# Cross-attention values kept in fp32 as two 64-column tiles, with the output projection inside the loop

## What is computed

```python
x = x + _L0_xattn_ref(_layernorm(x, axis=-1), ctx, ctx, ...)
x = x + _L0_ffn_ref(_layernorm(x, axis=-1), ...)
x = x + _L1_xattn_ref(ctx, _layernorm(x, axis=-1), mask, ...)
x = x + _L1_ffn_ref(_layernorm(x, axis=-1), ...)
# inside _L1_xattn_ref: 16 heads of 64; queries from x, keys and values from x and ctx together
...
out = out.transpose(0, 2, 1, 3).reshape(b, m, h * d)
return out @ Wout + bout
```

## Time and profile before

| what | value |
|---|---|
| median of 3 runs | 2465.91 us |
| profiled execution, its span | 2477.3 us |
| PE busy, weight loads busy | 2096.9 us (85%), 1762.3 us (71%) |
| DVE, ACT, POOL busy | 57%, 46%, 31% |
| the loop of pairs, from the first turn to the last fold | about 735.6 to 1942 us |
| the projection stage behind it | about 1942 to 2023 us |
| mean granted TensorE clock | 0.920 |

### The profile page before, as it was taken

How to read it: one execution, slowest core, us unless ns; L and a number is a source line. 1 busy time by engine, 2 the same in 40 slices (tenths; PEclk the granted TensorE clock), 3 DMA queues, 4 the chain that set the end, 5 groups by cost and what they waited for, 6 DMA issues and landing times. The chain is left out here.

```text
span 2477.3 us, 40299 instructions
## 1 busy us (share of the span) xinstructions
PE 2096.9 (85%) x13062; PEld 1762.3 (71%) x13063; DVE 1409.2 (57%) x3260; ACT 1135.1 (46%) x2179; POOL 764.3 (31%) x733
## 2 busy tenths in 40 slices
PE   5889539997159999999999999999998863799994
PEld 3569535664149988899998898988898753466772
DVE  4370236664638777777778877778877314321223
ACT  3443202221127667666677766666766311222220
POOL 2100002332164443454444444434541000122220
PEclk9898759999569999999999999999999985899997
DMA  5421351111200000000000000000000347111113
GB/s 192 142 85 55 142 190 37 44 47 41 81 20 1 16 17 16 2 16 16 16 16 16 1 16 17 16 17 1 16 10 9 106 152 263 41 34 31 32 34 113
DMA packets 85352, 131.30 MB, mean 53 GB/s; under 512 B 9825, under 2 KB 70943, under 8 KB 83115
## 3 DMA queue, kind: packets, MB, share of 16 engines
q1 hardware_dynamic: 74539, 106.16, 12.6%
q0 software_dynamic: 8320, 20.65, 2.9%
q10 hardware_dynamic: 2304, 2.10, 0.2%
HBM read 87.89 MB, written 40.80 MB: 52 GB/s over the span
## 5 line engine op out<-in xcount | busy, mean ns | idle before, releaser
L1585 ACT ACTIVATE a_probT<-a_slot 128x512 fp32r<-128x512 f32 (+1 forms) x512 | 320.4, 651 | 345.6 <-PE a_slot L1480 343.5
L1639 DVE TENSOR_REDUCE a_part_peak<-a_slot 128x1 f32<-128x512 f32 (+1 forms) x512 | 354.6, 731 | 154.4 <-PE a_slot L1471 150.0
L1686 DVE TENSOR_TENSOR a_probT<-a_slot,a_probT 128x512 fp32r<-128x512 f32 (+1 forms) x512 | 369.6, 753 | 18.2 <-ACT a_probT L1585 15.6
L1471 PE MATMUL a_slot<-a_KHL,a_QHL 128*128 128x512 f32 (+1 forms) x1536 | 337.2, 355 | 20.9 <-DVE a_probT L1686 14.4
L1494 PE MATMUL a_po<-a_probT,a_VHL 128*128 128x256 f32 (+1 forms) x2322 | 339.9, 291 | 11.1 <-DVE a_O L1705 4.4
L1471 PEld LDWEIGHTS a_slot<-a_KHL,a_QHL 128*128 128x128 f32 x1536 | 271.9, 190 | 94.9 <-DVE a_probT L1686 37.9
L1494 PEld LDWEIGHTS a_po<-a_probT,a_VHL 128*128 128x128 f32 (+1 forms) x2322 | 293.2, 189 | 24.6 <-issue 24.6
L1480 PE MATMUL a_slot<-ident,a_prob 128*128 128x128 f32 x2048 | 282.9, 282 | 10.6 <-issue 10.2
L1577 ACT ACTIVATE a_prob<-a_slot,a_npeak 128x1024 f32<-128x1024 f32 x256 | 284.6, 1112 | 1.0 <-DVE a_npeak L1641 1.0
L1480 PEld LDWEIGHTS a_slot<-ident,a_prob 128*128 128x128 f32 x2048 | 221.7, 142 | 11.3 <-issue 10.7
L1420 PE MATMUL a_side<-a_W,a_latT 128*128 128x128 f32 x1536 | 194.7, 281 | 14.1 <-DMA a_W<-in_L_xattn_Wkv_dram 9.6
(11 more groups left out here) (331 smaller groups left out, 3411.3 us busy)
## 6 DMA issues: line engine op xcount, KB each, us to landing
m_up<-_L_ffn_gate_up_proj_dram SPq DMA_DIRECT2D x8, 1024.0 KB
a_o_rows<-a_O SPq DMA_DIRECT2D x16, 512.0 KB, 3.5
a1o_o<-a_o_rows SPq DMA_DIRECT2D x16, 512.0 KB, 3.5
m_up<-in_L_ffn_W_dram SPq DMA_DIRECT2D x8, 1024.0 KB
m_down<-in_L_ffn_W_dram SPq DMA_DIRECT2D x8, 1024.0 KB
a_prob_dram<-a0p_zeros SPq DMA_DIRECT2D x4, 1632.0 KB, 10.6
a_dist_dram<-a_dist SPq DMA_DIRECT2D x4, 1632.0 KB, 8.2
a_band_prob<-a_prob_dram SPq DMA_DIRECT2D x4, 1632.0 KB, 7.0
```

The lines of the kernel that those rows point to most:

```text
L1471: ins = t_.matmul(out[:, lo:hi], q, KHL[:, pair.parity, h, part, lo:hi], start=part == 0, stop=part == 1)
L1585: a_.activation(probT[:, u // 2 % 2, 0, lo:hi, u % 2, :], slot[u % 2][:, lo * P:hi * P].rearrange("p (t q) -> p t q", q=P), ACT.Copy).then ...
L1639: v.tensor_reduce(part[:, i:i + 1], slot[u % 2][:, lo:hi], AX.X, ALU.max).then_inc(part_peaked, 1)
L1686: v.tensor_tensor(pT[:, 1], slot[u % 2][:, lo * P:hi * P].rearrange("p (t q) -> p t q", q=P), pT[:, 0], ALU.subtract).then_inc(probT_low, 1)
```

## The change

Seven edits, all in `layer1_attention` and in the host layout of its weights.

1. Values and turned probabilities are stored once, in fp32 (`V`, `probT`), not as high and low parts. ScalarE copies four of the nine turned blocks (`copy_first`) and VectorE the other five (`copy_rest`), each straight from PSUM; the subtractions go.
2. A group is now four units: two tiles of queries of both heads. `weigh` issues 18 fp32 matmuls of 256 columns: for each key tile one with head 0's 64 columns of values into partitions 0 to 63 of `po_t`, and one with head 1's into partitions 64 to 127. All 18 are issued in two bursts, eight behind the turn of unit u % 4 == 1 and ten behind that of u % 4 == 3, and ahead of the piece. Before, nine were issued with every unit, behind the piece.
3. The fold, `copy_outputs`, `O` and `o_rows` go. The row sums are inverted, widened to 64 columns each on VectorE, transposed by PE into `side` (`turn_sums`, u % 4 == 2), and copied by ScalarE (`copy_sums`); `normalise` then multiplies `po_t` in its transposed form.
4. The projection with Wout runs in the loop (`project_outputs`, u % 4 == 1): two fp32 matmuls of 256 columns per group into `side`, which VectorE adds to `xres` (`add_outputs`). The stage after the loop goes. bout is added to all of `xres` once, on GpSimd, behind its work for the first pair, and VectorE waits for that (`based`) ahead of the loop.
5. `side` is shared by pieces, sums and projections, so PE waits in `body` for `added` ahead of the piece of u % 4 == 1 and for `r_out` ahead of that of u % 4 == 2.
6. The three weights of a pair come as one contiguous DMA in place of three.
7. The loop has the first and the last pair of a batch written out, in place of the last two; three rounds of two stay.

```diff
-GROUPS = UNITS // 2
+GROUPS = UNITS // 4
+PARTS = [[], [8, 0, 1, 2], [], [3, 4, 5, 6, 7]]
...
-COPIED = ["Ka", "Kb", "Qa", "Qb"] + QUERY_TURNS
+COPIED = ["Ka", "Kb", "c", "Qa", "Qb", "Va", "Vb"] + QUERY_TURNS
...
             body(Pair(0, 0, 0, 0), True)
+            pool.wait_ge(w_out_loaded, 32)
+            g_.tensor_tensor(xres[:, :, :], xres[:, :, :], bout[:, :].unsqueeze(1).to_broadcast([P, TILES, E]),
+                             ALU.add).then_inc(based, 1)
...
-                for j in range(KT_TILES):
+                for j in PARTS[part]:
                     rows = P if j < S else CTX
-                    ins = t_.matmul(po_t, VHL[0:rows, pair.parity, j, gi % 2, :, :].rearrange("p a d -> p (a d)"),
-                                    probT[0:rows, gi % 2, part, j, :, :].rearrange("p t q -> p (t q)"),
-                                    start=part == 0 and j == 0, stop=part == 1 and j == S)
+                    for h in range(2):
+                        ins = t_.matmul(po_t[h * D1:(h + 1) * D1, :], V[0:rows, pair.parity, j, h, :], probT[0:rows, gi % 2, j, h, :],
+                                        start=j == PARTS[1][0], stop=j == PARTS[3][-1])
...
+            def turn_sums(pair, gi):
+                pe.wait_ge(widened, pair.g * GROUPS + (gi + 1))
+                for t in range(2):
+                    ins = t_.transpose(side[:, t * P:(t + 1) * P],
+                                       rwide[:, t, :, :].rearrange("p h d -> p (h d)"), ident[:, :])
+                ins.then_inc(r_turned, 1)
+
+            def project_outputs(pair, gi):
+                pe.wait_ge(normalised, pair.g * GROUPS + (gi + 1))
+                for t in range(2):
+                    ins = t_.matmul(side[:, t * E:(t + 1) * E], OT[:, t * P:(t + 1) * P],
+                                    Wout[:, bass.ds(pair.hp, 1), :].rearrange("p a n -> p (a n)"), start=True, stop=True)
+                ins.then_inc(y_done, 1)
...
                     turn(pair, u)
-                    if u % 2 == 0:
-                        fold_outputs(*(pair, u // 2 - 2) if u >= 4 else (before, u // 2 - 2 + GROUPS))
+                    if u % 4 == 1 and two_before[0]:
...
+                        project_outputs(owner, gi)
+                    if u % 4 == 2 and one_before[0]:
...
+                        turn_sums(owner, gi)
+                    if one_before[0]:
+                        weigh(*one_before, u % 4)
                     if after:
+                        if u % 4 == 1 and two_before[0]:
+                            pe.wait_ge(added, two_before[0].g * GROUPS + (two_before[1] + 1))
+                        if u % 4 == 2 and one_before[0]:
+                            pe.wait_ge(r_out, one_before[0].g * GROUPS + (one_before[1] + 1))
                         piece(after, PIECES[u])
-                    weigh(*(pair, u // 2 - 1) if u >= 2 else (before, GROUPS - 1), u % 2)
                     nxt = ahead(pair, u, 2)
                     if nxt[0]:
-                        pe.wait_ge(probT_low, (pair.g * UNITS + u) * 2 + 3)
+                        pe.wait_ge(probT_act, pair.g * UNITS + (u + 1))
+                        pe.wait_ge(probT_dve, pair.g * UNITS + (u + 1))
                         score(*nxt)
...
-            def copy_high(pair, u):
-
-                n = (pair.g * UNITS + u) * 2
-                for i, (lo, hi) in enumerate(((0, HALF), (HALF, KT_TILES))):
-                    act.wait_ge(turned, n + (i + 1))
-                    a_.activation(probT[:, u // 2 % 2, 0, lo:hi, u % 2, :], slot[u % 2][:, lo * P:hi * P].rearrange("p (t q) -> p t q", q=P),
-                                  ACT.Copy).then_inc(probT_high, 1)
+            def copy_first(pair, u):
+
+                act.wait_ge(turned, (pair.g * UNITS + u) * 2 + 1)
+                t, h = tile_head(u)
+                a_.activation(probT[:, u // 4 % 2, 0:HALF, h, u % 2 * P:(u % 2 + 1) * P],
+                              slot[u % 2][:, 0:HALF * P].rearrange("p (t q) -> p t q", q=P), ACT.Copy).then_inc(probT_act, 1)
+
+            def copy_sums(pair, gi):
+
+                act.wait_ge(r_turned, pair.g * GROUPS + (gi + 1))
+                a_.activation(rT[:, :], side[:, 0:2 * P], ACT.Copy).then_inc(r_out, 1)
...
                 for u in range(UNITS):
-                    copy_high(pair, u)
+                    one_before = group_before(pair, u, 1)
+                    copy_first(pair, u)
+                    if u % 4 == 2 and one_before[0]:
+                        copy_sums(*one_before)
 
                     early = after and PIECES[u] in ("K0a", "K0b", "Kc", "K1a", "K1b")
                     if early:
```

More of the change, by code:

```diff
@@ L1336, in body @@
                     load_weights((pair.hp + 2) % PAIRS if isinstance(pair.g, int) else pair.hp + 2, pair.parity)
[L1337 to L1341, removed]
             all_pairs(sp, body)
-            for i in range(2):
-                sp.wait_ge(o_stored[i], 16 * BATCH * PAIRS // 2 + 16)
+            sp.wait_ge(w_loaded[0], 16 * (BATCH * PAIRS // 2 + 1))
+            sp.wait_ge(w_loaded[1], 16 * (BATCH * PAIRS // 2))
         @block.gpsimd
@@ L1364, in body @@
                     tiles = nat.shape[1]
[L1366 to L1369, removed]
+                    pool.wait_ge(act_freed, count(pair, step, COPIED))
                     sq = square[:, 0:tiles, :]
@@ L1597, in body @@
             def body(pair):
-                after, before = pair.next(), pair.previous()
+                after = pair.next()
                 for u in range(UNITS):
-                    copy_high(pair, u)
+                    one_before = group_before(pair, u, 1)
+                    copy_first(pair, u)
+                    if u % 4 == 2 and one_before[0]:
+                        copy_sums(*one_before)
                     early = after and PIECES[u] in ("K0a", "K0b", "Kc", "K1a", "K1b")
@@ L1618, in _ @@
             v = nc.vector
-            dve.sem_inc(probT_low, 1)
-            dve.sem_inc(rsum_done, 1)
-            dve.sem_inc(row_summed, 5)
-            for h in range(2):
-                rows = slice(h * D1, (h + 1) * D1)
-                v.tensor_copy(fold[rows, :], ident[rows, rows]).then_inc(set_up, 1)
-            dve.wait_ge(set_up, NSET)
             for p in range(2):
@@ L1708, in _, with add_outputs @@
+            def add_outputs(pair, gi):
+                dve.wait_ge(y_done, pair.g * GROUPS + (gi + 1))
+                tile = pair.b * S + 2 * gi
+                x = xres[:, tile:tile + 2, :].rearrange("p t e -> p (t e)")
+                v.tensor_tensor(x, x, side[:, :], ALU.add).then_inc(added, 1)
             start = Pair(0, 0, 0, 0)
@@ L1803, in layer0_mixture @@
+            last = Pair(BATCH * PAIRS - 1, BATCH - 1, PAIRS - 1, (PAIRS - 1) % 2)
+            for gi in (GROUPS - 2, GROUPS - 1):
+                normalise(last, gi)
+                add_outputs(last, gi)
+            dve.wait_ge(added, BATCH * PAIRS * GROUPS)
+        attn.close()
 def layer0_mixture(nc, I, xres, ident):
@@ L1847, in lay_out @@
     out["ctx"] = a["ctx_1024"]
-    for n in ("Wq", "Wkv", "Wout"):
-        out[f"L1_xattn_{n}"] = a[f"L1_xattn_{n}"]
+    wq, wkv = (a[f"L1_xattn_{n}"].reshape(EC, P, -1, P) for n in ("Wq", "Wkv"))
+    by_pair = np.stack([wq, wkv[:, :, :PAIRS], wkv[:, :, PAIRS:]]).transpose(3, 2, 0, 1, 4)
+    out["L1_xattn_Wpair"] = by_pair[[p % PAIRS for p in range(PAIRS + 1)]]
+    out["L1_xattn_Wout"] = a["L1_xattn_Wout"]
     out["L1_xattn_bout"] = a["L1_xattn_bout"][None, :]
```

238 lines of the change are left out of this document (88 added, 150 removed).

## The result

The kernel before took 2469.44 us (median of 6 runs, 2465.64 to 2475.62), the changed kernel 2483.39 us (6 runs, 2478.97 to 2484.86). The ratio is 1.0053, 95% interval [1.0037, 1.0069]: slower by half a per cent. The forecast was 2475 on a median of 2466, so +9; it came to +14.

A forecast was written before the change was run, and what follows sets the result against it. PE's instruction list was taken as the bound. Stage -80, 15 pairs at +5.8 +87, last pair -3, tail +2, start +3 sum to +9: 2475 us on a median of 2466, range 2440 to 2545.

The forecast's parts named there:

- The stage after the loop: Projection after layer 1's loop: removed whole but for about 1 us of barrier, all of it counting, -80 us.
- Rival (a): In the bursts: the two heads' tiles don't run side by side, 15.5 us more per pair, +248, 2723 us; chance 0.11.
- Switches: PE changing between whole-array and half-array instructions around bursts: 0.25 us per burst, 2.0 per pair, 0 to 3.6.
- Rival (c): At the bursts: switches are free, -32 us, 2443; chance 0.21, shared with shorter waits than walked.
- Rival (b): In the bursts: half tiles' weight loads stand in the open, 7.8 us per pair, +124, 2599; chance 0.03.
- Work per pair: PE's instructions in a pair: bursts 15.6, projections 3.5, turned sums 0.9, switches 2.0, less 21.5 removed: +0.5 us.
- Turns behind early copies: Units 7 to 11: turns wait for exponentials behind ScalarE's early piece copies, 4.8 us per pair.
- The piece behind `turn_sums`: Units u % 4 == 2: the piece waits for the bank the sums are copied from, 0.69 four times, 2.8 us.
- Scores in short units: Units 8 and 12, without a burst: the score waits for VectorE's copy of five blocks, 0.65 twice, 1.3 us.
- The start: First pair: PE stands some 6 us for GpSimd's addition, 3 more at lower clock, less 5.5 of work: +3.5 us.
- The tail: After the last turn: last group's sums, matmuls, normalise, projection and add take 8.6 us against 6.8, +1.8.
- Rival (d): Units 8 to 12: PE's clock falls as it stands about a quarter of the time, over +200 us, 2690; chance 0.03.

The follow-up runs named there:

- The two edits of order: Two runs on the changed kernel: exponentials ahead of every piece copy, 2447.77 us; turned row sums moved ahead of the burst of 20, 2455.68 us.
- the kernel with the addition moved: The changed kernel with the output bias added to the residual on VectorE before its first copy of pair 0, not on GpSimd: 2473.28 us.
- the experiments: For 77.06: the changed kernel with exponentials ahead of every piece copy, sums ahead of the burst of 20 and bout on VectorE, 2424.20 us.

## Why the prediction was right, point by point

The time, 2475 against 2483, and the sum, +9 against +11 in the profiled executions, hold. So do the mechanisms that made it up. That the sum comes so close is partly luck, since sizes were off in both directions: the waits of a pair grew by 4.7 us (5.3 forecast) and the first pair saved 7.9 (5.5), but a pair's work grew by 1.2 (0.5) and the tail by 5.2 (1.8).

- **The stage after the loop.** -80 was -80.2.
- **The tiles run side by side.** The forecast was 1.8 and 2.2 us for a burst; it is 1.88 and 2.31. Rival (a) priced the case without overlap at 3.5 and 4.3; the order of issue alone brings 2.80 and 3.65, so part of that rival is one loop order away.
- **Switches.** Taken at 0.25 for each burst, measured 0.26, or up to 0.36 where a projected piece follows, three of eight. Rival (c), free switches, is out. The Trainium skill, "TensorEngine Tiling (Array Packing)", section "Key Properties", says that a change of tiling mode drains the engine; the trace agrees that it costs, with 0.10 on the way in and 0.16 on the way out (0.26 with the piece's 0.10), but not the 0.45 that I had tied to it.
- **Weight loads.** Rival (b) is out: 0.1075 per instruction leaves no room for an exposed load of 0.054. In the middle of a burst weight loads are under way 0.35 of 0.50 us while matmuls are under way all of it. The Trainium skill, "TensorE: Matmul & The Clock Gate", section "Part 3: Packing small matmuls — row/col tiling", says in its list of what overlaps that a load overlaps running matmuls only with a different row group; the halves here share their rows and differ in columns, and the trace disagrees with that sentence.
- **Work per pair.** Bursts with their entry 4 x (1.88 + 2.31) + 8 x 0.10 = 17.6, just the 15.6 + 2.0 forecast. Projections 0.86 each (0.96 from 1269.04 to 1270.00 less the entry), as forecast, so the address from a register costs nothing. Scores were priced too low, at 1.08 from one row. The changed kernel pays 1.14 to 1.18 wherever nothing delays the turn behind. But that is hardly new: in before the sixteen scores of a steady pair take 18.2 in all, six of them 1.06 to 1.08 and ten 1.16 to 1.20, most of these behind a wait, as here:

```profile
1236.77 1.34 PE L1471 MATMUL a_slot<-a_KHL,a_QHL 128*128 128x512 f32 x6
1237.94 1.09 PE L1480 MATMUL a_slot<-ident,a_prob 128*128 128x128 f32 x8
```

All distances of a steady pair, from each start to the next (before from 1506.84, after from 1638.46):

| PE's work, with the wait behind it | before | after |
|---|---|---|
| 16 turns | 16.6 | 17.0 |
| 16 scores | 18.2 | 22.7 |
| 16 pieces | 15.6 | 16.6 |
| weighing | 20.8 | 16.8 |
| folds | 3.1 | none |
| projections | none | 3.8 |
| turned sums | none | 3.4 |
| sum | 74.4 | 80.3 |

Taking out what exceeds the same step where nothing delays it leaves 70.7 of work before and 71.9 after: +1.2 where +0.5 was forecast (scores +0.2, pieces +0.8, the rest +0.2), and waits of 3.7 before, where the forecast had 4.7.

- **Waits per pair**, in the stretch above. Turns behind early copies: 1.10 + 1.09 + 1.09 + 0.75, and 0.19 in unit 8's place, 4.2 (forecast 4.8). The piece behind `turn_sums`: 0.86 less 0.23 for two transposes is 0.63, 2.5 in four (2.8). Scores in short units: 1266.67 - 1265.40 and 1286.80 - 1285.63, each less 0.42 for the piece, 1.6 (1.3). Together 8.3 against 8.9; the 1.1 for weight loads that I had added on top shows as no wait of its own. The two edits of order took out 2.6 and 1.6 of this, no more, since a part returns as the next wait.
- **The pair.** 81.08 against 81.5 forecast (81.4 without the short first distance), steady 80.26. The jumps of the loop were taken at 0.6 a pair, the listed 10.2 us; they cost 18.4 in all before and 14.5 after.
- **The start.** +3.7 against +3.5, but by parts that cancel. The hole and the slow stretch behind it were forecast at 9 and cost 9.4 (18.2 against 8.8 from the first turn to the first c, with and without GpSimd's addition): the addition took 8.82 us where I had worked out 7.5 from the earlier trace rows, PE's pause 7.3, not 6. The first pair gives back 7.9, not 5.5: 4.8 up to the first c (13.6 before, 8.8 with the addition moved) and 3.1 from there to the second. Not all of it is work: before starts its first turn at a lower clock (granted 0.59 from 735.59 to 740.00), the kernel with the addition moved at the full one (1.00 from 728.07 to 732.00). The other +2.2 lies ahead of the first turn and is no more than the scatter said above.
- **The tail** was mis-sized: +5.2 where I had +1.8. (My parts add up to 8.4, not 8.6, so +1.6.) I counted the work of the last group only. But the burst of the group before it, behind the turn of unit 15, comes ahead of that: 2.4 us and a wait of 0.7 for `normalise`:

```profile
2012.26 2.38 PE L1491 MATMUL a_po<-a_probT,a_V 128*64 128x256 f32 x20
2015.33 1.10 PE L1508 MATMUL a_side<-a1o_Wout,a_OT 128*128 128x256 f32 x4 [0.69 <-DVE a_OT L1717]
2017.21 0.44 PE L1500 MATMUL a_side<-ident,a_rwide 128*128 128x128 f32 x2 [0.78 <-DVE xres L1724]
2017.58 4.11 PE L1491 MATMUL a_po<-a_probT,a_V 77*64 77x256 f32 x36
```

- **The clock.** Rival (d) is out: the granted clock is 1.00 over the loop, and 1.00 from 1262 to 1287 us, the units with the waits of up to 1.1 us, where PE is busy 19.95 of 25.

So the change gains 80 us, and gives 81 back between the first c and the last pair. Its work costs some 1.2 us per pair more than the old; the other 4.7 of the 5.9 are waits, which its order of issue makes, and the experiments recover 3.2 (80.26 to 77.06) without touching its work, enough to turn half a per cent lost into two gained, with the hole at the start.

## What to carry to other kernels

When a group of matmuls is moved ahead of another step, look for whoever copies that step's result on an engine that also feeds the next unit: the same copy order was worth 0.8 us a pair with the step ahead of the matmuls and cost 2.6 with it behind. Two half-array tiles bring their full factor only if their instructions alternate closely in the list: in runs of 8 and 10 this kernel was 143 us slower. And compare two traces from the start of the changed phase: here the spans said +1.8 us and the medians +14.

## What the runs showed of the hardware

- Two 64-column fp32 tiles run side by side: 0.1075 us for each instruction of 256 columns against 0.216 for a whole-array one. With 2 or 4 instructions of one tile in a row this nearly holds (1.88 and 1.94 us for 16), with 8 or 10 only the last four of the first tile have the other beside them (2.80).
- Going to half-array tiles and back costs 0.26 us (0.10 in, 0.16 out), and 0.10 more where a projected piece follows.
- The same addition of 128 x 4096 fp32 numbers took 8.82 us on GpSimd and 4.41 on VectorE, and VectorE's wait for GpSimd's was 9.43.
- A jump back of the hardware loop adds 2.7 to 6.7 us to the distance it falls in, four times in each of the eleven traces here: 18.4 us in all before, 14.5 after.
